# A codebook search whose running maxima are turned earlier in a step, its coarse selections spread over three steps

## The chip, the cores and the metric

The kernel runs on one core of one Trainium2 chip. The metric is the device time of one execution in microseconds (us). A profile of one execution shows each engine's instructions: TensorE (PE, with its weight loads as PEld), VectorE (DVE), ScalarE (ACT), GpSimd (POOL) and the queue engine SyncE (SP).

## The reference, cut to what matters

An image pair x of shape (2, 128, 48, 48) passes four residual layers: dilated dynamic convolutions, a vector quantizer, a depthwise convolution with computed kernels, and two deformable convolutions. The change lies in the quantizer. With z the group-normalized image as 4608 rows of 128 channels, it finds for each row the nearest of 8192 codes and adds that code's row:

```
d = sum(z**2, axis=1, keepdims=True) + sum(codebook**2, axis=1) - 2 * z @ codebook.T
idx = argmin(d, axis=1)
z_q = codebook[idx]
```

Since the first term is the same for all codes of a row, the kernel looks for the largest z·c - c²/2.

## The kernel before, in words

**Tiling of the search.** The function `finale` holds the search and all that follows. The 4608 positions go in nine chunks n = 0 to 8 of 512 positions, and each chunk in four slices u = 0 to 3 of 128. The 8192 codes are eight groups of 1024; a chunk takes them in four steps s = 0 to 3 of two groups. A step has 16 units k: one unit is 128 codes against 512 positions, three bf16 matmuls (high and low halves, L1479 to L1481) into one of five PSUM slots in the order of the list `SLOT`. A unit that uses a slot again waits until VectorE (`dve_took`) or ScalarE (`act_took`) has taken the unit that was there before (`LAST`).

**Running maxima.** Units 0 and 1 start the two running maxima of a step, one for each group: ScalarE writes them with the bias -c²/2 (L1652). Units 2 to 15 are taken by VectorE (L1927): add the bias, keep the larger. After the step each of the two maxima holds, for 128 classes of codes, the best of eight codes, with classes in partitions and positions along the row.

**Turning.** To have positions in partitions, TensorE transposes the two maxima of a step behind two units of the next step (`turn`, L1367; unit numbers in `TURN_AT`, L1102), into one PSUM tile `turn_ps`. The first turn waits for VectorE's unit 14 of the step before, the second for unit 15 and until ScalarE has copied the first turn's result away (`keep`, L1581, copy in L1588). After four steps a chunk has 1024 maxima for each position.

**Coarse selection.** VectorE then finds, for each slice, the largest of the 1024 (`find`, MAX8 in L1760) and its place (`place_block`, FIND_INDEX8 in L1765). This is the work on chunk n-1 while chunk n is scored: the table `parts` (L1909) says behind which unit (s, k) each piece runs. `find` of slice 0 waits for the copy of the last turn (`kept`).

**Fine selection.** GpSimd's queue, in order, is: in step 1 `gather` of slices 0 and 1 (an indirect DMA, L2062, that fetches the chosen block of eight codes for each position, and waits for `found`), `multiply` of slices 0 and 1 (L2074); in step 2 gather 2, multiply 2, gather 3, fetch 0, multiply 3, fetch 1; in step 3 fetch 2 and 3. ScalarE sums the products of a slice in eight activations (`sum_products`, L1579): slice 0 at the end of step 1, slice 1 after units 0 and 1 of step 2, slice 2 at the end of step 2, slice 3 after units 0 and 1 of step 3. In steps 2 and 3 the two `keep` copies stand behind the sums of slices 1 and 3. VectorE finds the largest of eight sums (`fine_find`, L1771, at (2,4), (2,9), (3,2), (3,6) for slices 0 to 3) and its place one unit later (L1775). `fetch` (L2087) gathers the code's row. At the end of step 3 TensorE turns the four rows back (`turn_zq`, L1389) as soon as all have landed, and VectorE subtracts z (`subtract_z`, L1790).

**What is woven in.** In chunks 6 to 8 each engine's `lead` runs work of the next layers behind given units. Chunk 6 carries the depthwise convolution of the first image: nine taps on VectorE (L259) and 27 on TensorE (L273) in steps 2 and 3. In chunk 7, step 0, ScalarE normalizes the first image (L1627) ahead of its two `keep` copies; in step 1 TensorE turns this image in six pieces, ScalarE copies them (the last one behind the sums of slice 0), and behind unit 15 a convolution (L1404) waits for the last copy; in step 2 VectorE places and weighs the first sampling points (L1808 to L1838). Chunk 8 does the like for the second piece. At the end of chunk 7 GpSimd begins to issue the gathers of the deformable convolution (`rows`, L2147); in chunk 8 these stand between the gathers of the search in its queue.

Each engine runs its own instructions in the written order; semaphores are the only ties between them.

Of the kernel before, what the change touches and what calls it, by code (L numbers as in the profile page):

```python
# [1073 lines left out]
def finale(nc, tools, a, code_rows, x, xpad, ident, gm32, gm8, nc2, depthwise, between, places, out):  # L1074
# [24 lines left out]
    BY_DVE = NPR - BY_ACT  # L1099
    UNITS = NPX * STEPS * NPR  # L1100
    LOWER_FROM, LOWER_ADDED = 0, (10, 19, 28)
    TURN_AT = 9, 11  # L1102
    Z_TURN_AT = 12
    SLOT = [0, 1, 2, 3, 0, 4, 1, 2, 0, 3, 4, 1, 0, 2, 3, 4]

# [23 lines left out]
    with ExitStack() as ctx:  # L1129
# [236 lines left out]
        def _(pe):  # L1366
            def turn(S, h):  # L1367

                pe.wait_ge(dve_took, BY_DVE * (S + 1) - 1 + h)
                pe.wait_ge(kept, 2 * S + h)  # L1370
                for u in range(PXT):
                    mm = pe.transpose(turn_ps[:, u, :], run[S % 2][h][:, u * P:(u + 1) * P], ident)  # L1372
                mm.then_inc(turned, 1)
# [90 lines left out]
            def step(n, s):  # L1464
# [3 lines left out]
                for k in range(NPR):  # L1468
# [12 lines left out]
                    pe.matmul(o, cl[g][:, w], high, start=False, stop=True).then_inc(score_ready, 1)  # L1481
                    if k in TURN_AT and S:
                        turn(S - 1, TURN_AT.index(k))
                    if k == Z_TURN_AT and n and s == 0:
# [267 lines left out]
        def _(dve):  # L1752
# [115 lines left out]
            def lead(n, s, k):  # L1868
# [37 lines left out]
                if at == (2, 1, 14):  # L1906
                    weigh(0, 1, 1)

            parts = {(0, 12): (find, 0), (0, 14): (place_block, 0), (1, 2): (find, 1), (1, 4): (place_block, 1),  # L1909
                     (1, 6): (find, 2), (1, 8): (place_block, 2), (1, 10): (find, 3), (1, 12): (place_block, 3),  # L1910
                     **{(s, k + i): (part, u)
                        for s, k, u in ((2, 4, 0), (2, 9, 1), (3, 2, 2), (3, 6, 3))
                        for i, part in enumerate((fine_find, fine_place))}}
# [310 lines left out]
def program(nc, a, out):  # L2224
    tools = Tools(nc)
    with ExitStack() as ctx:
        x = tools.sb(ctx, "x", [P, B, HW])
        xpad = tools.sb(ctx, "xpad", [P, B * PADDED + WP])
        ident = tools.sb(ctx, "ident", [P, P])[:]
        gm32 = tools.sb(ctx, "gm32", [P, P])[:]  # L2230
        gm8 = tools.sb(ctx, "gm8", [P, P])[:]
        depthwise = Depthwise(tools, ctx, a, x, xpad, gm32)
        code_region = tools.sb(ctx, "code_region", [P, 10240])
        lead_region = tools.sb(ctx, "lead_region", [P, 7080])
        nc2 = tools.sb(ctx, "nc2", [P, GROUPS * PER])[:]
        gb = tools.sb(ctx, "gamma_beta", [P, 2])
        xy = tools.sb(ctx, "xy_sums", [P, N // CH // 2])
        moments = tools.sb(ctx, "in_moments", [P, B, 2])
        stats = tools.sb(ctx, "y_stats", [P, N // CH, 6])
        code_rows = nc.dram_tensor("code_rows", [CODES // PER, PER * ROW], F32).ap()  # L2240
        ch, cl = code_views(code_region[:])
        y = lead_region[:, 0:N]
        between = Between(tools, ctx, x.rearrange("p b n -> p (b n)"), y, stats, xy, moments, gb, gm32)
        layer0(nc, tools, a, x, xpad, gm32, gm8, ident, (ch, cl, nc2, code_rows), y, stats, xy, moments, gb, between)
        early_region = tools.sb(ctx, "early_region", [P, 5120])
        max_region = tools.sb(ctx, "max_region", [P, 10240])
        late_region = tools.sb(ctx, "late_region", [P, 5652])
        finale(nc, tools, a, code_rows, x, xpad, ident, gm32, gm8, nc2, depthwise, between,
               (code_region[:], lead_region[:], early_region[:], max_region[:], late_region[:]), out)
# [55 lines left out]
```

## Time and profile before

| | |
|---|---|
| three runs | 1625.98, 1627.93 (median), 1634.68 us |
| profiled execution, span from first to last instruction | 1625.7 us; its own time is not listed apart from the three runs, of which the lowest is 0.3 above the span |
| granted TensorE clock, mean | 0.864 |
| code search, first to last score matmul | 296.6 to 796.8 us |
| VectorE, TensorE, GpSimd, ScalarE busy | 1347.6, 1203.1, 1027.7, 432.4 us |

Reading: a row of the timeline gives the start and the length of an instruction (or of several alike, xN), and in brackets how long the engine was idle before it and what ended that. Lengths of neighbours overlap: VectorE's scoring units last 0.74 us and start 0.66 apart, a TensorE unit's three matmuls last 0.38 each and start 0.22 apart.

### The profile page before, as it was taken

To read this page: it belongs to the slowest core of one execution; us is meant where nothing else is said; L and a number is where in the kernel's file an instruction comes from. 1 tells how busy PE (TensorE), PEld (TensorE's weight loads), DVE (VectorE), ACT (ScalarE), POOL (GpSimd) and SP (SyncE) were. 2 spreads that over 40 slices of the span, in tenths; PEclk is the share of its full clock that TensorE was granted. 3 is DMA by queue.
4 is the path that set the end of the run, shared out by engine and by line. 5 is a ranking of instruction groups with operands and counts; after the bars stand their busy time and mean duration, and the time that the engine had idled before them with its cause. 6 is when DMAs were issued, how large, how long until landed. Compare 5 with 4: busy or idle time off the path is not lost. (4 is left out here: it accounts for less than half of the span.)

```text
span 1625.7 us, 19842 instructions
## 1 busy us (share of the span) xinstructions
PE 1203.1 (74%) x6050; PEld 749.5 (46%) x6094; DVE 1347.6 (83%) x1880; ACT 432.4 (27%) x1363; POOL 1027.7 (63%) x983
## 2 busy tenths in 40 slices
PE   5898999799888998888856676576655566545565
PEld 2454555344444444444445454454444344434444
DVE  5578898799999999898858989997787777888776
ACT  1241000124443343252456231221212211111111
POOL 6169798614443343136777677777777777777773
PEclk9889999799999999999978897787777867766777
DMA  5041000011211111054466797787877878777774
GB/s 170 14 154 55 1 0 0 15 48 44 59 55 44 34 46 55 5 172 133 147 219 190 224 289 208 210 270 228 249 208 229 251 229 250 209 234 210 210 209 145
DMA packets 111102, 232.65 MB, mean 143 GB/s; under 512 B 14676, under 2 KB 60500, under 8 KB 110748
## 3 DMA queue, kind: packets, MB, share of 16 engines
q0 software_dynamic: 58176, 191.30, 39.7%
q1 hardware_dynamic: 52828, 40.17, 7.8%
q8 instruction: 47, 0.77, 0.2%
q14 instruction: 51, 0.42, 0.1%
HBM read 205.15 MB, written 26.26 MB: 142 GB/s over the span
## 5 line engine op out<-in xcount | busy, mean ns | idle before, releaser
L2147 POOL DMA_INDIRECT code_region<-corners,lead_region x252 | 242.0, 960 | 77.9 <-issue 75.2
L1927 DVE SCALAR_TENSOR_TENSOR max_region<-score,nc,max_region 128x512 f32<-128x512 f32 x324 | 231.2, 742 | 33.3 <-PE score L1481 31.2
L772 POOL TENSOR_TENSOR prod_acc<-prod_acc,prod_pool 128x768 f32<-128x768 f32 (+8 forms) x118 | 172.0, 1457 | 61.5 <-DVE prod_pool L747 52.6
L2147 POOL DMA_INDIRECT early_region<-corners,lead_region x136 | 129.1, 949 | 41.3 <-issue 40.5
L1518 PE MATMUL score<-ident,code_region 128*128 128x128 f32 x540 | 95.7, 338 | 78.5 <-DVE code_region L1984 74.0
L2147 POOL DMA_INDIRECT max_region<-corners,lead_region x130 | 123.6, 951 | 41.3 <-issue 38.7
L2147 POOL DMA_INDIRECT late_region<-corners,lead_region x126 | 119.4, 948 | 43.2 <-issue 37.5
L1927 DVE SCALAR_TENSOR_TENSOR max_region<-lead_score,nc,max_region 128x512 f32<-128x512 f32 x180 | 132.5, 743 | 8.9 <-PE lead_score L1481 8.2
L1518 PEld LDWEIGHTS score<-ident,code_region 128*128 128x128 f32 x540 | 78.0, 175 | 94.9 <-DVE code_region L1984 87.8
L2062 POOL DMA_INDIRECT late_region<-code_rows,block_id x35 | 35.9, 1026 | 135.3 <-DVE block_id L1765 99.0
L1980 DVE TENSOR_TENSOR lead_score<-lead_score,code_region 128x768 f32<-128x768 f32 x78 | 75.4, 966 | 38.9 <-DMA code_region<-corners,lead_region 35.8
L2074 POOL TENSOR_TENSOR late_region<-late_region 128x1032 f32<-128x1032 f32 x32 | 70.3, 2195 | 44.7 <-DMA late_region<-code_rows,block_id 44.0
L1588 ACT COPY max_region<-turn_ps 128x512 f32<-128x512 f32 x72 | 42.1, 585 | 200.8 <-PE turn_ps L1372 200.8
L747 DVE TENSOR_TENSOR prod_pool<-spread,xpad 128x768 f32<-128x768 f32 (+8 forms) x118 | 90.1, 790 | 3.6 <-PE spread L670 3.0
L692 PE MATMUL y_ps<-prod_pe,w_scale 128*128 128x96 f32 (+7 forms) x360 | 89.4, 372 | 0.0
L1579 ACT ACTIVATE late_region<-late_region 128x129 f32<-128x129 f32 x280 | 82.5, 299 | 16.7 <-POOL late_region L2074 11.2
L1700 ACT COPY code_region<-score 128x384 f32<-128x384 f32 x72 | 34.3, 477 | 177.3 <-PE score L1518 171.5
L670 PE MATMUL spread<-wta,sel_a 108*128 x352 | 74.7, 315 | 7.1 <-DVE prod_pool L747 3.3
L1518 PE MATMUL score<-ident,early_region 128*128 128x128 f32 x310 | 49.7, 315 | 38.1 <-DVE early_region L1984 26.9
L747 DVE TENSOR_TENSOR prod_pe<-spread,xpad 128x752 f32<-128x752 f32 (+7 forms) x92 | 56.9, 630 | 25.0 <-PE spread L670 24.4
L1496 PE MATMUL turn_ps<-code_region,max_region 128*128 128x256 f32 x216 | 72.2, 486 | 6.3 <-ACT code_region L1700 6.3
L1984 DVE TENSOR_TENSOR code_region<-lead_score,code_region 128x768 f32<-128x768 f32 x78 | 74.7, 957 | 2.7
(298 smaller groups left out, 3089.0 us busy)
## 6 DMA issues: line engine op xcount, KB each, us to landing
corners<-lead_region SPq DMA_DIRECT2D x72, 192.0 KB
corners<-lead_region SPq DMA_DIRECT2D x8, 576.0 KB
code_rows<-codes_n SPq DMA_DIRECT2D x8, 516.0 KB, 3.8
codes_t<-in_codes_t SPq DMA_DIRECT2D x8, 512.0 KB, 3.7
codes_n<-in_codes SPq DMA_DIRECT2D x8, 512.0 KB, 4.1
code_region<-corners,lead_region POOLq DMA_INDIRECT x252, 3.7
x<-in_x SPq DMA_DIRECT2D x2, 1152.0 KB, 6.4
out<-x SPq DMA_DIRECT2D x4, 576.0 KB, 3.1
```

What stands on the lines that cost most here:

```text
L670: mm = pe.matmul(to, sel[:, kk, :], v, start=True, stop=True)
L692: mm = pe.matmul(dst, w_scale[:, o["i"] + 1, :], src.rearrange("p (r w) -> p r w", r=rows), start=False, stop=last, skip_group_check=True)
L747: dve.tensor_tensor(to, w, v, ALU.mult).then_inc(prod_ready, 1)
L772: pool.tensor_tensor(to, to, v, ALU.add).then_inc(pooled, 1)
L1496: mm = pe.matmul(yps, w_tap[j // B][:, 3 * g + k, :], turned_x[g][:, k, :], start=g + k == 0, stop=g + k == 4)
L1518: mm = pe.matmul(tps[g][:, k * P:(k + 1) * P], quad(T, 3 * g + k)[:, c * P:(c + 1) * P], ident, start=c == low, stop=c == CORNERS - 1, is_ ...
L1579: act.activation(v, v, ACT.Identity, accum_out=fine[:, u, j:j + 1]).then_inc(summed, 1)
L1927: dve.scalar_tensor_tensor(r, score[SLOT[k]], nc2[:, m:m + 1], r, ALU.add, ALU.max).then_inc(dve_took, 1)
L1980: return dve.tensor_tensor(upper_ps, bc(w[:, k, 0:2], P), q[:, k, 0:2], ALU.mult)
L1984: dve.tensor_tensor(q[:, k, 2:4], upper_ps, q[:, k, 2:4], ALU.add).then_inc(halved, 1)
L2074: pool.tensor_tensor(v, v, zb, ALU.mult).then_inc(multiplied, 1)
L2147: pool.indirect_dma_start(quad(T, k), None, table[j].rearrange("n s c -> n (s c)"), bass.IndirectOffsetOnAxis(index[j % B][:, at:at + 1], 0))\
```

## The change

The turns of a step's maxima move from behind units 9 and 11 of the next step to behind units 6 and 8. In the table of VectorE's pieces the coarse selections get new places; the fine ones stay.

```diff
-    TURN_AT = 9, 11
+    TURN_AT = 6, 8
...
-            parts = {(0, 12): (find, 0), (0, 14): (place_block, 0), (1, 2): (find, 1), (1, 4): (place_block, 1),
-                     (1, 6): (find, 2), (1, 8): (place_block, 2), (1, 10): (find, 3), (1, 12): (place_block, 3),
+            parts = {**{at: (part, u) for u, ats in enumerate((((0, 9), (0, 13)), ((1, 2), (1, 6)), ((1, 10), (1, 14)), ((2, 3), (2, 7))))
+                        for at, part in zip(ats, (find, place_block))},
                      **{(s, k + i): (part, u)
                         for s, k, u in ((2, 4, 0), (2, 9, 1), (3, 2, 2), (3, 6, 3))
                         for i, part in enumerate((fine_find, fine_place))}}
```

| slice | find, before | place, before | find, after | place, after |
|---|---|---|---|---|
| 0 | (0, 12) | (0, 14) | (0, 9) | (0, 13) |
| 1 | (1, 2) | (1, 4) | (1, 2) | (1, 6) |
| 2 | (1, 6) | (1, 8) | (1, 10) | (1, 14) |
| 3 | (1, 10) | (1, 12) | (2, 3) | (2, 7) |

## Rows read from the trace of the kernel before

**Rows 1.** The page, busy time of each engine over the span.

```profile
PE 1203.1 (74%) x6050; PEld 749.5 (46%) x6094; DVE 1347.6 (83%) x1880; ACT 432.4 (27%) x1363; POOL 1027.7 (63%) x983
```

**Rows 2.** Windows, chunk 3, steps 0 to 3 and their sum.

```profile
core 0: us, PE busy (x) PEld busy (x) DVE busy (x) ACT busy (x) POOL busy (x), PEclk, DMA share, GB/s
447.95:460.26 12.31, 12.26 (x63) 6.38 (x63) 11.73 (x18) 3.07 (x6) 1.62 (x2) 1.00 0.00 1
460.26:476.44 16.18, 11.87 (x55) 4.84 (x55) 16.18 (x25) 5.74 (x27) 8.02 (x8) 1.00 0.35 99
476.44:487.37 10.93, 10.83 (x54) 5.46 (x55) 9.77 (x22) 6.27 (x32) 7.42 (x8) 1.00 0.20 57
487.37:499.04 11.67, 11.62 (x60) 6.10 (x60) 10.40 (x22) 4.79 (x21) 3.77 (x6) 1.00 0.07 17
sum 51.09, PE 46.57 PEld 22.79 DVE 48.09 ACT 19.86 POOL 20.83; mean PE 11.64 PEld 5.70 DVE 12.02 ACT 4.96 POOL 5.21
```

**Rows 3.** Groups by line, VectorE, chunk 3: busy us, mean ns, idle.

```profile
L1760 DVE MAX8 best<-max_region 128x8 f32<-128x1024 f32 x4 | 4.9, 1222 | 0.0
```

**Rows 4.** Timeline, VectorE, chunk 3: start us, us, what, idle before.

```profile
458.47 1.23 DVE L1765 FIND_INDEX8 block_id<-best,max_region 128x8 uint32<-128x1024 f32 x1
...
473.34 1.22 DVE L1765 FIND_INDEX8 block_id<-best,max_region 128x8 uint32<-128x1024 f32 x1
...
480.59 0.74 DVE L1927 SCALAR_TENSOR_TENSOR max_region<-lead_score,nc,max_region 128x512 f32<-128x512 f32 x1
...
490.87 0.16 DVE L1771 MAX8 fine_best<-fine 128x8 f32<-128x8 f32 x1
```

**Rows 5.** Timeline, GpSimd, chunk 3.

```profile
460.60 0.96 POOL L2062 DMA_INDIRECT late_region<-code_rows,block_id  x1 [10.95 <-DVE block_id L1765]
...
479.34 1.01 POOL L2062 DMA_INDIRECT late_region<-code_rows,block_id  x1 [0.15 <-issue]
...
483.78 2.20 POOL L2074 TENSOR_TENSOR late_region<-late_region 128x1032 f32<-128x1032 f32 x1 [0.93 <-DMA late_region<-code_rows,block_id]
```

**Rows 6.** DMA issues from 395 to 600 us: count, median us to landing.

```profile
late_region<-code_rows,block_id POOLq DMA_INDIRECT x16, 4.4
```

**Rows 7.** Timeline, GpSimd, chunk 2.

```profile
428.19 1.02 POOL L2062 DMA_INDIRECT late_region<-code_rows,block_id  x1
...
433.62 2.19 POOL L2074 TENSOR_TENSOR late_region<-late_region 128x1032 f32<-128x1032 f32 x1 [1.92 <-DMA late_region<-code_rows,block_id]
```

**Rows 8.** Timeline, ScalarE, chunk 3: first and last of eight sums.

```profile
487.30 0.30 ACT L1579 ACTIVATE late_region<-late_region 128x129 f32<-128x129 f32 x1
...
489.55 0.20 ACT L1579 ACTIVATION_READ_ACCUMULATOR late_region<-late_region 128x1 f32 x1
```

**Rows 9.** Timeline, TensorE, ScalarE and VectorE, chunk 7.

```profile
681.22 0.35 PE L149 MATMUL lead_score<-n_mean_var,gm 128*128 128x2 f32 x2 [3.35 <-DVEq L144]
...
687.50 2.31 ACT L1627 ACTIVATE y_first<-x,n_shift,n_scale 128x2304 f32<-128x2304 f32 x1 [2.39 <-DVEq L182]
...
690.43 0.63 PE L1372 MATMUL turn_ps<-ident,max_region 128*128 128x128 f32 x4 [1.52 <-DVE max_region L1927]
...
691.74 0.75 DVE L1927 SCALAR_TENSOR_TENSOR max_region<-lead_score,nc,max_region 128x512 f32<-128x512 f32 x1 [0.79 <-PE lead_score L1481]
...
708.67 2.10 PE L1404 MATMUL lead_score<-xpad,lead_region 128*32 128x384 f32 x18 [0.42 <-issue]
...
725.52 2.20 DVE L1825 TENSOR_SCALAR lead_region<-lead_region 128x54 f32<-128x54 f32 x1
```

**Rows 10.** Windows, chunk 7, start of step 0 (columns as in rows 2).

```profile
681.44:685.06 3.62, 3.62 (x11) 1.27 (x11) 3.34 (x8) 0.15 (x1) 2.53 (x2) 0.53 0.02 5
```

**Rows 11.** Timeline, VectorE and GpSimd, chunk 8.

```profile
775.11 0.31 DVE L1825 TENSOR_SCALAR lead_region<-lead_region 128x54 f32<-128x54 f32 x1
...
781.24 0.99 POOL L2062 DMA_INDIRECT late_region<-code_rows,block_id  x1
...
781.40 0.74 DVE L1927 SCALAR_TENSOR_TENSOR max_region<-lead_score,nc,max_region 128x512 f32<-128x512 f32 x1
```

**Rows 12.** Windows from 745.5 to 873 us (columns as in rows 2).

```profile
745.50:873.00 127.50, 91.67 (x509) 58.63 (x509) 99.51 (x172) 60.11 (x235) 95.72 (x99) 0.87 0.62 190
```

## The prediction

> **What bounds the kernel now.** I read the page first: VectorE is the busiest engine of the span, TensorE next [rows 1]. The change touches the code search alone, which runs from 296 to 798 us. So I took one chunk of 512 positions (n = 3) and asked for the busy time of its four steps [rows 2]. The reader is to see that the bound changes inside the chunk. Step 1, with three of the four coarse selections, lasts 16.18 us and VectorE is busy for all of it, while TensorE loses 4.3. In steps 0, 2 and 3 TensorE is busy to within 0.1 and VectorE waits: 0.58 + 1.16 + 1.27 = 3.0 us a chunk. TensorE needs 46.6 and VectorE 48.1 of the chunk's 51.1. By the code chunks 1 to 5 do the same work; in chunks 6 to 8 work of the next layers is woven in. From 745 us on GpSimd issues gathers with hardly a break: 99 instructions in 127.5 us [rows 12].
>
> **The change, part by part.**
>
> *What moves.* A coarse selection is a maximum and a find, 1.22 us each [rows 3, 4]. Slice 3's pair (2.4 us) goes from step 1 to units 3 and 7 of step 2, and slice 0's maximum three units earlier, which the earlier turn allows. Nothing is added or removed: 16 units, eight transposes and the same copies stay in each step. The turns wait for VectorE's last two units of the step before; unit 5, which TensorE computes ahead of unit 6, uses the PSUM slot of the very last of these, so the turn at 6 adds no wait for VectorE. Price: 0 in an ordinary step; below, chunk 7.
>
> *What the spreading could free.* If nothing else were late, step 1 would shrink by slice 3's 2.4 us and step 2, where VectorE waits 1.16, would grow by about 1.3, so up to 1.1 a chunk comes free at once, and 3.0 if every gap closed.
>
> *What is late next.* The last selection starts a chain: GpSimd gathers the chosen block, multiplies it, ScalarE sums it, VectorE takes the fine maximum at unit 6 of step 3. Before, slice 3's find ended at 473.34 + 1.22 = 474.56 and the fine maximum came at 490.87, 16.3 us later [rows 4]: much slack. Now the find stands behind unit 7 of step 2. The VectorE work up to there is the same set in another order, and VectorE had no gap in step 1, so the find ends about where unit 8 started before: 480.6 [rows 4]. Then, step by step:
> - find to gather: slice 0's find ended at 458.47 + 1.23 = 459.70 and its gather started at 460.60 [rows 4, 5]: 0.90, so 481.5 (before: 479.34);
> - gather to multiplication, with the landing between: 483.78 - 479.34 = 4.44 [rows 5], median landing 4.4 [rows 6]: 485.95;
> - multiplication: 2.20 [rows 5]: 488.15;
> - the eight sums: 489.55 + 0.20 - 487.30 = 2.45 [rows 8]: 490.6, and about 0.1 to VectorE's start.
>
> That is 490.7 against 490.87: the fine maximum, which all of step 3 and the row fetch hang on, stays where it was. Only 0.1 to 0.2 of the chunk is freed; the 1.1 turns into a wait of VectorE for ScalarE's sums. ScalarE also copies the turned maxima behind these sums, so TensorE's second turn of step 3 waits a little too. I take -0.1 a chunk, -0.5 for chunks 1 to 5. Bounds: -0.4 (a landing of 4.1, 0.3 under the median) and +1.0 (chunk 2's gather took 433.62 - 428.19 = 5.43 to its multiplication [rows 7]), so -2 to +5.
>
> *Chunk 6.* Steps 2 and 3 carry 27 convolution taps on TensorE and nine on VectorE. That makes both steps long, and the chain can hide in them. I take 0; bounds -1 (step 1 ends earlier) and +1.5 (a tap on VectorE meeting a multiplication).
>
> *Chunk 7, step 0.* Here the turn at 8 does add a wait. ScalarE normalizes the image for 2.31 us from 687.50 before it copies the first turned half, and the second turn waits for that copy: before, at unit 11, it started at 690.43 after 1.52 idle [rows 9]. With the turn behind unit 8, units 9, 10 and 11 are queued behind it. VectorE now gets unit 9 when it got unit 12 (691.74, rows 9), three units behind: 3 x 0.66 = 2.0. Slice 1's find moves two units down (+1.3): its gather stands ahead of the first multiplication on GpSimd, whose sums stand ahead of the last copy of turned x on ScalarE, for which the convolution at the end of step 1 waited already (708.67 after 0.42 idle, rows 9). So 1.3 more reaches step 2. And TensorE then stands still for over 3 us; before, after the stop of 3.35 that ended at 681.22, the granted clock was 0.53, about the 1.2 GHz level, for 3.62 us [rows 9, 10]. Such a stretch costs half of itself, 1.8; the maximum of slice 0 (1.2), for which VectorE needs no new unit, covers a part: +0.8. Against it: at 725.52 a small operation of the weights took 2.20 while GpSimd multiplied, and 0.31 in chunk 8 [rows 9, 11]: 1.9 that another order may miss; I take a quarter, -0.5. Sum 2.0 + 1.3 + 0.8 - 0.5 = +3.6; bounds +0.8 (the lock missed, the clock kept, half of the 1.3 hidden) and +5.
>
> The Trainium skill ("SBUF — State Buffer", section on the two sides) calls the port pair that VectorE and GpSimd share an exclusive lock, held for the whole instruction. By that the 2.20 is all lock, and the trace agrees (2.20 against 0.31); the sum with the whole 1.9 missed would be +2.9 in place of +4.3.
>
> *Chunk 8 and the end of the search.* GpSimd's stream is what counts here. Slice 3's gather started at 781.24 without a wait; its find now ends where unit 8 of step 2 started, 781.40 [rows 11], plus 0.90: 782.3, so 1.1 of wait, and its followers inherit it. I take +1.2; bounds 0 (the find comes early as VectorE's own gaps close) and +2.5 (the sums late for the fine maximum too).
>
> *Sum:* -0.5 + 0 + 3.6 + 1.2 = +4.3. The profiled span is 1625.7, so 1630.0. The median of the three runs, 1627.9, lies 2.2 above it, so I forecast **1632.2 us**. Added bounds give -2 to +14.
>
> **The rivals.**
>
> *Faster: VectorE's gaps close.* Over chunks 1 to 8 that would be 8 x 3.0 = 24: 1604. For it: VectorE is the busiest engine, and step 1's overload is what the spreading takes apart [rows 2]. Against it: the chain above lands at 490.7, and steps 0 and 3 have TensorE without a gap. The Trainium skill ("Perfetto Trace Analysis", section Identifying the Most-Contended Engine) would have the engine of the highest occupancy optimized first, which here means closing those gaps; the trace agrees on the occupancy (48.1 of 51.1), but no row shows that the gaps can close.
>
> *Slower: the gather decides.* It hangs on slice 3's landing: from some 4.5 us on, each further one delays the fine maximum, the fetch of the rows and TensorE's last turn one to one. With chunk 2's 5.43 in each of chunks 1 to 6 that is +6.0, with 3.6 + 1.2 behind it +10.8: 1638.7. For it: one such gather in the stretch; against it: the median of 16 is 4.4 [rows 6].
>
> *No effect: the later stage swallows it.* If what follows the search has slack of its own, a shift of 4 us is lost in it and the change does nothing that shows: 1628. For it: in the span as a whole no engine is busy over 83% [rows 1]. Against it: GpSimd's stream from 745 on [rows 12], and that the stages behind start from the same events, all late alike.
>
> **How the numbers follow.** Forecast 0.60, faster rival 0.04, slower rival 0.17, no effect 0.19. Some 0.5% (8 us) is what a measurement here tells from no change: slower means over 1636.1. That takes the slower rival nearly whole and a tenth of the forecast: 0.20. Faster, under 1619.8, is its rival and a little of the rest: 0.05. Same: 0.75. The range 1624 to 1640 reaches from the forecast's lower bound, with the spread of the runs, over the no-effect case to the slower rival.
>
> **What would show it.** Steps of chunk 3 near 12.3, 13.9, 12.3 and 12.4 in place of 12.3, 16.2, 10.9 and 11.7; a wait of VectorE for the sums of late_region, some 1 us before slice 3's fine maximum; the second turn of chunk 7's step 0 waiting for ScalarE over 3 us, then a low clock; GpSimd waiting for block_id before slice 3's gather in chunk 8. The prediction is wrong if chunks fall under 50.5 us, if they rise over 52, or if chunk 7 is not longer.

## The result, and the profile after

The changed kernel takes 1636.87 us (median of 20 runs, 1631.89 to 1638.23), the kernel before 1627.22 (20 runs): ratio 1.0052, 95% interval 1.0043 to 1.0061, so +8.5 us (7.0 to 9.9; the two medians differ by 9.65). The forecast was +4.3 on the span. The time lies 4.7 above the 1632.2 forecast and inside the range. The interval reaches to both sides of the 0.5% from which the prediction called a kernel slower (chance 0.20; same, 0.75), so these runs do not settle which of the two came. The waits forecast for chunks 1 to 5, 7 and 8 were found in the trace. The sum is half of what came, because the terms of chunks 6 and 8 were too small; that of chunk 7 fits, but by luck, as told below.

The page of the changed kernel, busy time of each engine; it answers to [rows 1].

```profile
PE 1204.1 (74%) x6050; PEld 750.3 (46%) x6094; DVE 1346.2 (82%) x1880; ACT 432.0 (26%) x1363; POOL 1027.7 (63%) x983
```

The engines are busy for the same time in a span longer by 9.9 (1635.6 against 1625.7): what was added is waiting, so the stages must be read one by one. Windows of the changed kernel, steps 0 to 3 of chunk 3, as in [rows 2].

```profile
448.79:461.13 12.34, 12.10 (x62) 6.17 (x62) 11.73 (x18) 3.07 (x6) 1.98 (x3) 1.00 0.01 1
461.13:474.99 13.86, 12.13 (x58) 5.60 (x59) 13.86 (x22) 4.84 (x21) 6.46 (x6) 1.00 0.26 77
474.99:487.25 12.26, 10.83 (x52) 4.97 (x52) 12.03 (x25) 7.03 (x36) 6.32 (x8) 1.00 0.34 94
487.25:499.67 12.42, 11.80 (x60) 6.01 (x60) 10.53 (x21) 4.79 (x21) 6.07 (x8) 1.00 0.06 16
```

Step 1 lost 2.3 us, steps 2 and 3 took 2.1 of it back; VectorE has 1.9 without work in step 3 where it had 1.27. Next comes the chain behind slice 3's find. As in the prediction, "find" means FIND_INDEX8, which the code calls `place_block` and the tables call the place. The rows are from the timeline of chunk 3 (VectorE, GpSimd, ScalarE, TensorE), and stand against [rows 4, 5, 8]:

```profile
480.33 1.22 DVE L1765 FIND_INDEX8 block_id<-best,max_region 128x8 uint32<-128x1024 f32 x1
482.44 1.01 POOL L2062 DMA_INDIRECT late_region<-code_rows,block_id  x1 [0.43 <-ACT late_region L1579]
486.80 2.20 POOL L2074 TENSOR_TENSOR late_region<-late_region 128x1032 f32<-128x1032 f32 x1 [0.84 <-DMA late_region<-code_rows,block_id]
489.02 0.31 ACT L1579 ACTIVATE late_region<-late_region 128x129 f32<-128x129 f32 x1 [1.74 <-POOL late_region L2074]
491.62 0.17 DVE L1771 MAX8 fine_best<-fine 128x8 f32<-128x8 f32 x1 [0.79 <-ACT late_region L1579]
492.10 0.63 PE L1372 MATMUL turn_ps<-ident,max_region 128*128 128x128 f32 x4 [0.56 <-ACT max_region L1588]
```

The chunk starts 0.84 later than in the rows of before. With that added, the prediction's working gives 481.4 for the end of the find, then 482.3, 486.8, 489.0 and 491.5; the rows have 481.55, 482.44, 486.80, 489.02 and 491.62. The gather's row names ScalarE as the one that released it, but the sums that it waits for, slice 1's, had ended at 477.3; what came last is the find, 0.89 earlier. The last row is TensorE's second turn, which waits for ScalarE's copy behind the sums.

Windows of chunk 7, steps 0 to 3: first the kernel before, then the changed kernel.

```profile
681.84:696.72 14.88, 13.30 (x63) 6.77 (x63) 13.45 (x27) 8.11 (x11) 2.53 (x2) 0.90 0.01 1
696.72:712.89 16.17, 15.18 (x86) 7.41 (x87) 16.17 (x24) 7.10 (x27) 8.02 (x8) 1.00 0.93 271
712.89:731.20 18.31, 13.17 (x62) 6.16 (x62) 15.50 (x36) 10.07 (x54) 8.05 (x8) 0.95 0.49 142
731.20:743.69 12.49, 12.44 (x60) 6.28 (x60) 10.64 (x21) 2.41 (x4) 3.21 (x5) 0.94 0.05 12
```

```profile
685.53:702.37 16.84, 13.32 (x64) 6.75 (x63) 13.44 (x27) 8.13 (x11) 2.87 (x3) 0.91 0.00 1
702.37:719.78 17.41, 14.97 (x85) 7.53 (x86) 14.03 (x21) 6.96 (x27) 6.88 (x7) 1.00 0.85 252
719.78:739.66 19.88, 12.87 (x64) 6.08 (x64) 18.33 (x38) 10.18 (x54) 8.84 (x10) 1.00 0.44 131
739.66:751.02 11.36, 11.31 (x59) 5.93 (x59) 10.39 (x22) 2.41 (x4) 3.17 (x5) 1.00 0.05 13
```

Chunk 7 of the changed kernel, timeline of TensorE, ScalarE and VectorE, answering to [rows 9].

```profile
684.91 0.35 PE L149 MATMUL lead_score<-n_mean_var,gm 128*128 128x2 f32 x2 [3.36 <-DVEq L144]
691.19 2.31 ACT L1627 ACTIVATE y_first<-x,n_shift,n_scale 128x2304 f32<-128x2304 f32 x1 [2.38 <-DVEq L182]
694.11 0.63 PE L1372 MATMUL turn_ps<-ident,max_region 128*128 128x128 f32 x4 [3.47 <-ACT max_region L1588]
695.43 0.75 DVE L1927 SCALAR_TENSOR_TENSOR max_region<-score,nc,max_region 128x512 f32<-128x512 f32 x1 [2.77 <-PE score L1481]
715.59 2.10 PE L1404 MATMUL lead_score<-xpad,lead_region 128*32 128x384 f32 x18 [1.84 <-issue]
727.83 2.06 DVE L1808 TENSOR_SCALAR lead_region<-lead_region 128x54 f32<-128x54 f32 x1
734.42 2.08 DVE L1825 TENSOR_SCALAR lead_region<-lead_region 128x54 f32<-128x54 f32 x1
```

The second turn waits 3.47 us for ScalarE, as forecast. Windows of the changed kernel behind TensorE's two stops of step 0, answering to [rows 10]: the clock is low after the first, at full speed after the second.

```profile
685.12:688.75 3.63, 3.63 (x12) 1.40 (x12) 3.35 (x8) 0.14 (x1) 2.54 (x2) 0.53 0.00 0
694.11:698.58 4.47, 4.42 (x26) 2.73 (x27) 3.15 (x5) 1.36 (x3) 0.00 (x0) 1.00 0.02 4
```

Chunk 8, timeline of GpSimd and VectorE: two rows of the kernel before, slice 0's gather and the first of the small operations, that stand beside [rows 11]; then the changed kernel.

```profile
763.07 0.94 POOL L2062 DMA_INDIRECT late_region<-code_rows,block_id  x1 [0.30 <-DVE block_id L1765]
774.87 0.21 DVE L1823 TENSOR_TENSOR lead_region<-lead_region 128x54 f32<-128x54 f32 x1
```

```profile
770.42 0.95 POOL L2062 DMA_INDIRECT late_region<-code_rows,block_id  x1 [0.30 <-issue]
779.18 2.19 POOL L2074 TENSOR_TENSOR late_region<-late_region 128x1032 f32<-128x1032 f32 x1 [1.18 <-DMA late_region<-code_rows,block_id]
779.89 1.56 DVE L1823 TENSOR_TENSOR lead_region<-lead_region 128x54 f32<-128x54 f32 x1
788.85 1.22 DVE L1765 FIND_INDEX8 block_id<-best,max_region 128x8 uint32<-128x1024 f32 x1
790.96 0.99 POOL L2062 DMA_INDIRECT late_region<-code_rows,block_id  x1 [2.84 <-ACT late_region L1579]
```

Gather 3 waits 2.84 and starts 20.54 behind gather 0 (770.42 to 790.96); before, it was 18.17 (763.07 to 781.24). It starts 0.89 after the find, which is later by more than its move: the small operation L1823 stood still until GpSimd's multiplication was over, 1.56 in place of the 0.21 that it took before.

Chunk 6, step 1 by windows: the kernel before, the changed kernel, and a kernel whose chunk 6 is word for word that of before (the third experiment).

```profile
617.53:638.14 20.61, 14.83 (x70) 8.02 (x70) 17.68 (x31) 10.40 (x36) 7.99 (x9) 0.92 0.28 78
```

```profile
618.47:641.38 22.91, 19.88 (x78) 10.49 (x78) 15.74 (x28) 11.54 (x44) 6.98 (x7) 0.78 0.22 60
```

```profile
614.99:637.24 22.25, 16.72 (x71) 9.50 (x70) 17.93 (x32) 10.41 (x36) 8.08 (x9) 0.85 0.25 72
```

Here lies the largest gap between forecast and trace: chunk 6 went from 80.64 to 83.85, +3.2 where 0 was forecast. But the third row shows the code of before at 22.25, with a granted clock of 0.85: the profile of before had caught step 1 at 0.92.

### The profile page after: what moved, and what is told of

The parts are those of the page before. It is cut to its first block and busy times, and to the rows that moved or that the text cites. A ratio compares the mean times of both kernels' runs of the same rounds, so it can differ in the third digit from the quotient of the medians.

```text
span 1635.6 us, 19842 instructions
## 1 busy us (share of the span) xinstructions
PE 1204.1 (74%) x6050; PEld 750.3 (46%) x6094; DVE 1346.2 (82%) x1880; ACT 432.0 (26%) x1363; POOL 1027.7 (63%) x983
## 5 line engine op out<-in xcount | busy, mean ns | idle before, releaser
L1518 PE MATMUL score<-ident,early_region 128*128 128x128 f32 x310 | 50.2, 316 | 38.8 <-DVE early_region L1984 29.2
L1518 PE MATMUL score<-ident,late_region 128*128 128x128 f32 x270 | 47.9, 340 | 37.5 <-DVE late_region L1984 37.5
```

Of the source, the lines that this page charges most:

```text
L1518: mm = pe.matmul(tps[g][:, k * P:(k + 1) * P], quad(T, 3 * g + k)[:, c * P:(c + 1) * P], ident, start=c == low, stop=c == CORNERS - 1, is_ ...
```

## Experiments

Each kernel was timed in five rounds beside the kernel before; the ratio is to it, with a 95% interval. Kernels 1 to 4, 5 to 8 and 9 to 12 are three series, each with runs of the kernel before of its own (medians 1626.72, 1627.82 and 1628.72 us). Chunk lengths run from VectorE's first scoring unit of a chunk to that of the next, in one profiled execution; "g3 - g0" is the start of slice 3's gather behind slice 0's in chunk 8.

| kernel | ratio | chunk 3 | chunk 6 | chunk 7 | g3 - g0 |
|---|---|---|---|---|---|
| before | | 51.08 | 80.64 | 61.85 | 18.17 |
| changed | 1.0052 (1.0043 to 1.0061) | 50.89 | 83.85 | 65.50 | 20.54 |
| 1 new in chunks 0 to 5 | 1.0004 (0.9991 to 1.0016) | 50.88 | 82.28 | 62.05 | 18.08 |
| 2 new in chunk 6 | 1.0008 (0.9994 to 1.0021) | 51.08 | 83.01 | 60.65 | 18.53 |
| 3 new in chunk 7 | 1.0042 (1.0026 to 1.0057) | 51.08 | 82.27 | 65.25 | 18.29 |
| 4 new in chunk 8 | 1.0014 (1.0002 to 1.0026) | 51.09 | 82.29 | 62.36 | 20.99 |
| 5 less spread, chunks 1 to 5 | 0.9965 (0.9952 to 0.9978) | 49.88 | 82.26 | 62.03 | 17.75 |
| 6 chunk 7, late turns in step 0 | 1.0010 (0.9995 to 1.0026) | 51.09 | 82.29 | 61.72 | 17.82 |
| 7 chunk 7, slice 1 early | 1.0015 (1.0006 to 1.0025) | 51.08 | 82.26 | 65.33 | 17.91 |
| 8 chunk 8, weighing later | 1.0000 (0.9987 to 1.0013) | 51.08 | 82.27 | 62.49 | 19.85 |
| 9 turns only | 1.0020 (1.0001 to 1.0038) | 51.12 | 85.12 | 64.16 | 18.07 |
| 10 spread only | 1.0021 (1.0007 to 1.0035) | 50.21 | 82.28 | 65.82 | 20.86 |
| 11 changed, copy first | 1.0027 (1.0013 to 1.0042) | 51.01 | 82.86 | 61.64 | 20.94 |
| 12 best | 0.9949 (0.9931 to 0.9966) | 49.90 | 84.85 | 57.49 | 17.97 |

All take the unit numbers from functions of the chunk, so that one chunk can have the old and another the new; OLD and NEW are the coarse places of before and of the change. Line numbers lie 5 to 9 higher in their profiles.

```diff
-                    if k in TURN_AT and S:
-                        turn(S - 1, TURN_AT.index(k))
+                    if k in turn_at(n, s) and S:
+                        turn(S - 1, turn_at(n, s).index(k))
...
-                    if n and (s, k) in parts:
-                        part, u = parts[s, k]
+                    if n and (s, k) in parts[n]:
+                        part, u = parts[n][s, k]
```

### 1 to 4: one stage at a time

```diff
+    turn_at = lambda n, s: (6, 8) if n < 6 else (9, 11)
+    coarse_at = lambda n: NEW if n < 6 else OLD
```

(2: `n == 6`, 3: `n == 7`, 4: `n == 8`.)

> New turns and new coarse places in chunks 0 to 5 only, the old ones in chunks 6 to 8. Theory (the chain gather, multiplication, sums, fine maximum replaces VectorE's overload at equal length): chunks 1 to 5 stay at 50.9 to 51.1 us each, 0.1 under before, so the whole at -0.5 us, ratio 0.9997. Rival (the early turns and the spreading cost time in every chunk, by TensorE's short stops): each chunk 0.3 to 1 us longer, +2 to +5, ratio 1.001 to 1.003. Rival (VectorE's gaps close over the chunks): -3 or more, ratio under 0.998.

> New in chunk 6 only. Theory: what was forecast as 0 is really there. In the changed kernel's trace chunk 6 is 3.2 us longer (80.64 to 83.86), 2.3 of it in step 1, because TensorE runs longer at the low granted clock behind the small matmuls of the computed kernels, so unit 11, the kernels, the diagonals and the first tap come late: +3, ratio 1.0019, and TensorE's mean clock in step 1 under that of before. Rival (the forecast's 0 was right and the 3.2 is the chance of one execution, or was handed down from the earlier chunks): within 0.5 us of before, ratio 1.0000 to 1.0003.

> New in chunk 7 only. Theory (forecast): +3.6 us, ratio 1.0022; step 0 longer by 2.0, for TensorE's second turn waits over 3 us for ScalarE, step 1 by 1.3 for slice 1's gather comes two units later. Rival (the later stage swallows it, GpSimd's gathers of the next layer being the bound from there): chunk 7 3 to 4 longer in the trace, yet under 0.5 us at the end, ratio 1.0000 to 1.0003. Rival (mishaps of the lock: the steps of VectorE meet other multiplications): chunk 7 longer in step 2 and not in steps 0 and 1, between 1 and 5 us.

> New in chunk 8 only. Theory (forecast): GpSimd's gather of slice 3 waits 1.1 us for its place and hands it on: +1.2 us, ratio 1.0007. Second reading, from the changed kernel's trace: that gather starts 2.4 us later against the gather of slice 0, since step 2, which takes slice 3's pair in, is longer by 1.9 while step 1 is shorter by 1.1 only: +2.2, ratio 1.0014. Rival (hidden by GpSimd's stream of gathers of the next layer): 0, ratio 1.0000.

Measured: +0.7, +1.3, +6.8 and +2.3 us, together 11.1 where the whole change costs 8.5; each is uncertain by 2 to 2.5, so they add up within that. Chunks 1 to 5 sum to 254.6 us in the trace of 1, 0.8 under before. Chunk 7 is 3.4 longer in the trace of 3, near the 3.6 forecast: in steps 0 (16.84 against 14.88) and 1 (17.41 against 16.18), and 1.3 more in step 2 less 1.1 in step 3. In six executions with the code of before chunk 7 took 60.65 to 62.49, so the 65.25 here and the 65.50 of the changed kernel lie clear of it. The timed runs of 3 rose by more, 4.2 to 9.3 by the interval. Its profiled execution took 1630.97 us where the median of its 12 runs is 1633.47, which makes up part of that; the rest stays open. Chunk 8 follows the second reading (+2.3 for the +2.2 expected).

For chunk 6 neither reading came: the timed runs give +1.3 (-1.0 to +3.4), between them. The traces tell more. With the code of before chunk 6 took 82.26 to 82.29 in seven further executions, and 80.64 and 84.85 in one each (the kernel before and the twelfth run). New, it took 83.85, 83.01 and 82.86. So 1.6 of the 3.2 was the profile of before. Of the rest, 0.9 belongs to the early turns: step 0 took 16.32 to 16.33 and step 3 22.13 to 22.14 in all ten executions with the turns behind 9 and 11 there (the tenth run, with the places new, among them), against 16.77 to 16.79 and 22.58 in the changed kernel, the second and the ninth. (The eleventh, with early turns too, has the 22.58, and 18.20 in step 0 at a clock of 0.81.) Step 1 cannot be told apart by code: it goes with the granted clock, 20.5 to 20.6 us at 0.92, 22.1 to 22.3 at 0.85, 22.9 at 0.78 and 24.2 to 24.8 at 0.72, with old and new pieces alike.

### 5: how late may slice 3 be?

```diff
+    turn_at = lambda n, s: (9, 11)
+    coarse_at = lambda n: OLD[:3] + (((1, 14), (2, 4)),) if n < 6 else OLD
+    fine_at = lambda n: ((2, 7, 0), (2, 13, 1), (3, 2, 2), (3, 6, 3)) if n < 6 else FINE
```

> Chunks 1 to 5 only, and the turns stay behind units 9 and 11: of the coarse pieces only slice 3's move, its maximum from (1,10) to (1,14) and its place from (1,12) to (2,4), three units earlier than the change has it; the fine pieces of slices 0 and 1 go to (2,7) and (2,13). Theory (the length of the chain from slice 3's find to its fine maximum decides how much of the spreading pays): the find ends some 2 us earlier against the step, VectorE's 1 us wait for the sums is gone, chunks 1 to 5 take 49.9 us each against 51.1 before and 50.9 in the changed kernel; together -6 us, ratio 0.9963. Rival (chunks cannot get shorter, for TensorE or ScalarE is late by as much, whatever VectorE does): 50.8 to 51.1 each, 0 to -1.5 us. Rival (the landing of the gathers scatters and takes it back): some chunks at 51 or more.

Windows of its chunk 3:

```profile
443.30:455.61 12.31, 12.31 (x64) 6.38 (x63) 11.73 (x17) 3.07 (x6) 1.62 (x2) 1.00 0.01 1
455.61:470.59 14.98, 12.24 (x58) 5.21 (x57) 14.98 (x22) 5.67 (x26) 8.01 (x8) 1.00 0.32 83
470.59:481.52 10.93, 10.80 (x54) 4.98 (x52) 10.90 (x24) 6.33 (x33) 7.00 (x7) 1.00 0.28 89
481.52:493.19 11.67, 11.67 (x61) 6.11 (x60) 10.41 (x22) 4.79 (x21) 4.21 (x6) 1.00 0.06 17
```

49.89 a chunk: step 1 lost 1.2, and neither step 2 nor step 3 gave any of it back. The wait for the sums is gone: slice 3's fine maximum stands in the timeline without one.

```profile
485.02 0.16 DVE L1776 MAX8 fine_best<-fine 128x8 f32<-128x8 f32 x1
```

So the rival that chunks cannot get shorter falls. But the run differs from the changed kernel in two things, the later turns and slice 3's smaller move, and the tenth run (below) parts them: with the late turns alone chunks 2 to 5 take 50.2 to 50.4, against 50.9 to 51.0 with the early ones. Of the 1.1 us between the changed kernel and this one, 0.6 goes with the turns, and 0.4 with slice 3's smaller move and the pieces moved along with it, which take VectorE's wait for the sums away.

### 6, 7 and 11: what chunk 7 pays for

```diff
+    # 6
+    turn_at = lambda n, s: (6, 8) if n == 7 and s else (9, 11)
+    coarse_at = lambda n: OLD[:1] + NEW[1:] if n == 7 else OLD
+    # 7
+    turn_at = lambda n, s: (6, 8) if n == 7 else (9, 11)
+    coarse_at = lambda n: (NEW[0], OLD[1], *NEW[2:]) if n == 7 else OLD
```

> New in chunk 7 only, but in its step 0 the turns stay behind units 9 and 11 and slice 0's pair at (0,12) and (0,14). Theory (the 2.0 us of step 0 are the three units queued behind the second turn, which waits for ScalarE's normalization): step 0 back at 14.9 us, step 1 still at 17.4, chunk 7 at 63.4 in place of 65.4, and the whole about 2 us or more under the kernel with all of chunk 7 new: +1.6 to +4. Rival (the wait is only moved on to the next stop): step 1 grows by what step 0 loses, chunk 7 at 65.

> New in chunk 7 only, but slice 1's place stays at (1,4). Theory (step 1 is longer since slice 1's gather, which stands ahead of the first multiplication, goes out two units later, and with it come the sums, the last copy of turned x and the convolution): step 0 stays at 16.8 us, step 1 loses 1.3 and VectorE's waits in it go, chunk 7 at 64.1. Rival (step 1 is long because ScalarE and TensorE were put out of step by the stop in step 0): step 1 stays at 17.4.

The run with late turns in step 0 missed its expectation (63.4): chunk 7 is back at 61.72. Against the third run not only the 2.0 of step 0 went, but 1.6 of step 2 too, where the granted clock is 1.00 and was 0.91. Windows of steps 1 to 3 of the sixth, then the seventh kernel:

```profile
696.80:714.22 17.42, 15.10 (x87) 7.55 (x86) 14.04 (x21) 6.98 (x27) 7.64 (x7) 1.00 0.87 252
714.22:732.28 18.06, 12.92 (x65) 6.06 (x64) 16.51 (x37) 10.06 (x54) 8.34 (x10) 1.00 0.48 140
732.28:743.64 11.36, 11.36 (x60) 5.88 (x59) 10.40 (x22) 2.55 (x6) 3.17 (x5) 1.00 0.07 19
```

```profile
696.69:712.79 16.10, 15.08 (x87) 7.53 (x86) 14.03 (x22) 6.97 (x27) 6.96 (x7) 1.00 0.92 268
712.79:732.61 19.82, 14.92 (x63) 6.87 (x62) 16.60 (x37) 10.11 (x54) 8.76 (x10) 0.87 0.46 132
732.61:745.19 12.58, 12.58 (x61) 6.32 (x60) 10.71 (x22) 2.41 (x4) 3.18 (x5) 0.93 0.06 17
```

The trace of the seventh missed its expectation (64.1): step 1 is shorter by 1.3, as the gather of slice 1 goes earlier, yet steps 2 and 3 are longer by as much, at a granted clock of 0.87 and 0.93, and the chunk stays at 65.33. Its timed runs say otherwise: +2.4 us (1.0 to 4.1) against the third run's +6.8 (4.2 to 9.3). So whether the 1.3 of step 1 is a cost by itself stays open.

The eleventh kernel leaves the whole change in place and moves ScalarE's first copy ahead of the normalization:

```diff
                 if at == (1, 0, False):
-                    norm_.act(act, 0)
+                    act.wait_ge(norm_.var_ready, 1)
+                    act.sqrt(norm_.tmp[:], norm_.var[:]).then_inc(norm_.rooted, 1)
+                    keep(n * STEPS - 1, 0)
+                    act.wait_ge(norm_.affine, 1)
                     act.activation(y0[:], x[:, 0, :], ACT.Identity, bias=norm_.shift[:], scale=norm_.scale[:])\
...
-                    for h in range(2):
+                    for h in range((n, s) == (L0 + 1, 0), 2):
                         keep(S - 1, h)
```

> The whole change, and in chunk 7 ScalarE copies the first turned half between the square root and the normalization of the image, which stands idle there for 2.4 us, in place of behind it. Theory (the second turn's wait for that copy is the whole price of chunk 7): the wait of over 3 us before the second turn is gone, step 0 near 14.2 to 14.9 us, chunk 7 near 61.7 in place of 65.4, ratio to before 1.003 in place of 1.0052. Rival (TensorE and VectorE run into the next wait, for the normalized image or the convolution): chunk 7 at 64 or more, ratio 1.005.

Its timeline, ScalarE and TensorE:

```profile
683.72 0.59 ACT L1593 COPY max_region<-turn_ps 128x512 f32<-128x512 f32 x1 [0.58 <-PE turn_ps L1377]
684.82 0.60 PE L1377 MATMUL turn_ps<-ident,max_region 128*128 128x128 f32 x4
685.52 2.31 ACT L1635 ACTIVATE y_first<-x,n_shift,n_scale 128x2304 f32<-128x2304 f32 x1 [1.22 <-DVEq L182]
```

The second turn no longer waits, step 0 takes 14.86 and chunk 7 61.64; the whole is at 1.0027, half of the change's cost. Two different ways to take the wait away give the same chunk, and the timed runs fall with it (the sixth 5 us under the third, the eleventh 4 under the changed kernel). That step 0's 2.0 us are the wait is shown. The 1.6 to 1.9 that step 2 gave back came about differently: in the sixth by the clock, in the eleventh because the first small operation of the sampling points took 0.17 us where in the changed kernel it stood still for 2.06 (the row at 727.83). That the wait brings these about is not shown, and the seventh kernel's runs fall by 4 with the wait left in.

### 8: the small operations of chunk 8

```diff
-                if at == (2, 1, 14):
+                if at == (2, 2, 4):
                     weigh(0, 1, 1)
```

with `n == 8` new as in the fourth run.

> New in chunk 8 only, and the eight small operations that weigh the sampling points move from behind (1,14) to behind (2,4), away from the second multiplication. Theory (of the 2.5 us that slice 3's gather comes later against slice 0's, 1.35 are the first small operation standing still while GpSimd multiplies): no small operation over 0.5 us in steps 1 and 2, gather 3 some 19.3 us behind gather 0, against 18.2 before and 20.5 to 21.0 in the changed chunk; the whole at +1, ratio 1.0006. Rival (the 2.5 is all slice 3's place, that comes four units later): gather 3 still 20.5 or more behind gather 0, ratio 1.0014.

Its timeline, VectorE and GpSimd:

```profile
761.78 0.94 POOL L2068 DMA_INDIRECT late_region<-code_rows,block_id  x1 [0.30 <-issue]
775.71 0.20 DVE L1828 TENSOR_TENSOR lead_region<-lead_region 128x54 f32<-128x54 f32 x1
781.63 0.99 POOL L2068 DMA_INDIRECT late_region<-code_rows,block_id  x1 [1.78 <-ACT late_region L1584]
```

The operation took 1.73 in the fourth run and takes 0.20 here; gather 3 stands 19.85 behind gather 0 against 20.99. So 1.1 of the delay goes with it, half a microsecond short of the expected 19.3. The rest fits slice 3's later place, which no run moved alone. The whole comes to 1.0000; that it is under the expected 1.0006 lies within the interval.

### 9 and 10: the two lines of the change apart

```diff
+    # 9
+    turn_at = lambda n, s: (6, 8)
+    coarse_at = lambda n: OLD
+    # 10
+    turn_at = lambda n, s: (9, 11)
+    coarse_at = lambda n: OLD[:1] + NEW[1:]
```

> Only the first line of the change: turns behind units 6 and 8 in all chunks, the coarse places as before. Theory (the turns cost only where the second one waits for ScalarE, in step 0 of chunk 7): chunks 1 to 5 at 51.1 us, chunk 6 within 0.5, chunk 7 3.4 longer (step 0 by 2.0), chunk 8 within 0.3; +3.5 us, ratio 1.0022. Rival (the turns are free, and the cost of chunk 7 comes from the places, which keep VectorE off the taps): within 0.5 us, ratio 1.0000 to 1.0003.

> Only the second line of the change: slices 1, 2 and 3 at their new places in all chunks, the turns behind units 9 and 11 and slice 0 where it was. Theory (the spreading costs in chunk 8 by the lock and by slice 3's later gather, gives 0.1 in each of chunks 1 to 5, and nothing in chunk 7): chunks 1 to 5 at 51.0, chunk 6 within 0.7, chunk 7 near 61.7 with step 1 at 17.4, chunk 8's gather 3 some 20.7 us behind gather 0 against 18.2 before; +2.5 us, ratio 1.0015. Rival (the parts add up otherwise: the early turns are what makes the spreading dear): within 0.5 us.

Each costs some 3.3 us, together 6.7 where both cost 8.5; each is uncertain by 2 to 3, so that is within it. The turns alone make chunk 7 2.3 longer in the trace, 1.95 of it in step 0, less than the 3.4 expected, and chunk 6 took 85.12 with the clock at 0.72 in step 1. For the spreading two things were not expected. Without the early turns the spreading does give something in an ordinary chunk, 50.21 against 51.08. Its step 3:

```profile
487.17:498.94 11.77, 11.77 (x61) 6.00 (x60) 10.44 (x22) 4.91 (x21) 5.64 (x8) 1.00 0.06 17
```

TensorE has no gap in it, where the changed kernel loses 0.6 at the second turn (the row at 492.10 above): behind unit 11 this turn comes after ScalarE's copy, behind unit 8 before it. And chunk 7 took 65.82 although no turn waits in its step 0: step 1 has 18.86 at a clock of 0.91, step 2 19.36 at 0.87. So the spreading alone can make chunk 7 as long as the wait does; it did so here and not in the sixth run, and one trace each does not tell which of the two is the rule. The timed runs fit both traces. Of the tenth's +3.4 (1.1 to 5.7), chunks 1 to 5 give -2.9 and gather 3 in chunk 8 +2.7 by its trace, which leaves some +3.6 for chunk 7, an estimate; the sixth, with chunk 7 alone new, costs 1.6 (-0.8 to 4.2).

### 12: a version that is faster than both

```diff
+    turn_at = lambda n, s: (6, 8) if n == L0 + 1 else (9, 11)
+    coarse_at = lambda n: OLD[:3] + (((1, 14), (2, 4)),) if n < 6 else \
+        (((0, 12), (0, 13)), ((0, 14), (0, 15)), ((1, 9), (1, 11)), ((2, 2), (2, 3))) if n == 7 else OLD
+    fine_at = lambda n: ((2, 7, 0), (2, 13, 1), (3, 2, 2), (3, 6, 3)) if n < 6 else FINE
```

with ScalarE's copy first, as in the eleventh.

> A version from both readings: in chunks 1 to 5 slice 3 moved by three to eight units only, as in the run with 49.9 us a chunk; in chunk 7 the early turns with ScalarE's copy ahead of the normalization, slices 0 and 1 selected at the end of step 0 (behind 12 to 15), slice 2 at (1,9) and (1,11), slice 3 at (2,2) and (2,3); chunks 6 and 8 as before. Theory (in chunk 7 the convolution at the end of step 1 hangs on slice 1's gather, so an earlier one lets it start earlier): chunks 1 to 5 -6 us, chunk 7 2 to 3 shorter than the 61.9 of before, together -8, ratio 0.995. Rival (chunk 7 is held by the stores of the turned image and by the low clock in its steps 2 and 3): -6, ratio 0.9963.

1620.22 us, ratio 0.9949 (0.9931 to 0.9966): -8.3 us against before, where the changed kernel has +8.5. Windows of its chunk 7, steps 0 to 3:

```profile
677.58:693.89 16.31, 15.90 (x79) 8.21 (x78) 15.67 (x30) 9.03 (x12) 3.71 (x4) 0.92 0.07 8
693.89:706.81 12.92, 12.55 (x73) 5.92 (x72) 11.63 (x18) 6.05 (x24) 6.85 (x6) 1.00 1.08 323
706.81:723.70 16.89, 14.26 (x65) 6.96 (x64) 14.94 (x37) 9.08 (x49) 8.00 (x8) 0.90 0.56 160
723.70:735.07 11.37, 11.37 (x60) 5.93 (x59) 10.40 (x23) 3.32 (x11) 3.19 (x5) 1.00 0.05 13
```

57.49 in place of 61.9, the 2 to 3 us expected and more, and 49.9 in each of chunks 2 to 5; chunk 6, with the code of before, took 84.85 in this execution. The rival's 0.9963 lies inside the interval too; what speaks against it is the trace, where step 1 of chunk 7 takes 12.92 in place of 16.17.

## Why the prediction was right, and where its working was off

**Chunks 1 to 5 (-0.5).** Right: 0.4 less in the changed kernel, 0.8 in the first experiment, and the chain came to within 0.1 us at every link. Off in one point: that the fine maximum's place fixes the length of the chunk. In the tenth run it comes at the same place (491.45 in a chunk that starts at 448.73), VectorE waits for the sums as long (0.69 against 0.79), and the chunk is 0.7 shorter; TensorE had run ahead by then. In the changed kernel the second turn's wait takes that back. The prediction named this wait and gave it no price, and it put the early turns at 0 in an ordinary step. By themselves they cost nothing there (51.12 in the ninth run), but they take back most of the 0.7 that the spreading gives alone.

**Chunk 6 (0).** The largest gap between the sum and the trace, +3.2. Half of it is the one execution that the sum was made against. Of the other half, 0.9 is the early turns in steps 0 and 3, which the prediction put at nothing, and the rest goes with the clock of step 1. Against the usual 82.3 the three executions with chunk 6 new are 0.6 to 1.6 longer, about as far as the upper bound given (+1.5). What the working left out is that the length of step 1 goes with TensorE's granted clock: the rows above have it at 0.92, 0.85 and 0.78, with 20.61, 22.25 and 22.91 us, and the run with the turns alone had 0.72 and 24.21. Whether the change shifts this clock is not shown, since the code of before had 0.92, 0.85 and, in the twelfth run, 0.72. VectorE's time without work in this step grew from 2.9 to 7.2 us; 2.4 of that is slice 3's pair, moved on, and the step gained nothing by it, since VectorE then waits for TensorE.

**Chunk 7 (+3.6).** Right in its first cause, the second turn behind unit 8: step 0 is 1.96 longer, three units, as worked. That the sum fits too (65.50 - 61.85 = 3.65) is luck, since the other terms are off and cancel. The 1.3 of step 1 is there (1.23), but step 3 gives 1.1 back, at a clock of 1.00 where the profile of before had 0.94; whether saving the 1.3 gains anything, trace and timed runs of the seventh kernel answer differently. The 0.8 for the clock is not there: it stood at 1.00 behind the second stop. The -0.5 has the wrong sign: the changed kernel has two small operations held up for over 2 us (the rows at 727.83 and 734.42) where before one took 1.45 and one 2.20, which is 0.5 more. For step 2, into which slice 3's pair moves, the sum had no term. It is 1.6 longer: VectorE's busy time in it grew by 2.8, by the pair's 2.4 and this 0.5, and only 1.3 of that went into VectorE's waits. In the third run, with one such operation, it is 1.3 longer at a clock of 0.91.

**Chunk 8 (+1.2).** The mechanism was right, the size was half: gather 3 is 2.4 later against gather 0. What is missing is L1823, which now meets a multiplication and takes 1.35 longer; with this meeting taken away, the eighth run got 1.1 back. The prediction had allowed for a meeting missed in chunk 7, and for none gained in chunk 8. The description of the kernel before calls semaphores the only ties between the engines; here is another, since no semaphore ties this operation to the multiplication. The Trainium skill ("SBUF — State Buffer", section on the two sides) says that the engine which comes second to the shared port pair is blocked for the whole instruction of the first; the trace agrees: the operation ended at 781.45, the multiplication at 781.37.

**The rivals.** "The gather decides" did not happen: in the changed kernel's chunks 1 to 5 no landing took over 4.52 us, and no chunk over 51.12. "VectorE's gaps close" is wrong for this change, and the fifth run shows that a smaller move closes 1.2 of the 3.0 in each chunk. "The later stage swallows it" is wrong: GpSimd's first gather of the last chunk's selection starts 9.5 later (818.90 against 809.38), and the span is 9.9 longer.

What remains between the traces (+9.9) and these terms (-0.4 + 3.2 + 3.65 + 2.4 = 8.85): the search began 1.4 later in the changed kernel's profile and its chunk 0 took 0.5 less. The start lay anywhere from 297.7 to 302.7 in fourteen profiles, ahead of anything that the edit touches. With this 1.4, and 1.6 from the profile of before in chunk 6, the traces' 9.9 holds chance; the timed +8.5 is the better measure.

## What to carry to other kernels

Work taken off an overloaded step helps until the chain that starts with it (here find, gather, multiplication, sums, fine maximum) arrives later than before: work out that chain link by link, and move the piece only as far as its slack. Give every wait that you name a price, too: the unpriced wait of the second turn took 0.6 us a chunk here. An edit to a table that all stages share must be worked out for the stages with other work woven in: here it gave 0.4 us in the five plain ones and cost 7 to 9 in the three mixed ones, and one copy put ahead of a 2.3-us operation gave half of the whole change's cost back. Before a term is judged against a profile, look at the same unchanged stage in several executions.

## What the runs showed of the hardware

The same code of chunk 6's step 1 ran at a mean granted clock of 0.92 in one execution (20.61 us), 0.85 in seven (22.25) and 0.72 in one (24.82). That the stop ahead of a stretch doesn't settle it is seen in chunk 7, where a stop of 3.36 us was followed by 0.53 and one of 3.47 by 1.00. Small VectorE operations of 0.2 us took up to 2.2 us where they fell into one of GpSimd's multiplications, and ended within 0.1 us after it. Which one was hit differed from kernel to kernel, with pieces moved in quite another step.
